# Keys made once a batch for the second cross attention, and weighted sums three chunks behind the scores

## The reference

```
# first (layer 0): 16 heads; the context is layer-normed, heads of 32 features
# second (layer 1):
qh = (q @ Wq + bq).reshape(B, LQ, 16, 8)      # 8 features a head
kh = (k @ Wk + bk).reshape(B, LKV, 16, 8)
vh = (v @ Wv + bv).reshape(B, LKV, 16, 8)
attn = softmax(qh kh^T / sqrt(8));  out = (attn vh) @ Wo + bo
```

## Time and profile before

| | us |
|---|---|
| median of 3 runs | 667.15 (667.14 to 670.14) |
| profiled execution | 664.66 |
| its span, first to last instruction | 662.9 |
| TensorE busy | 621.5 (94%) |
| VectorE, GpSimd, ScalarE busy | 493.9, 379.3, 353.0 |

### The profile page before, as it was taken

One profiled execution on the slowest core, in us unless ns is written; L12 is line 12 of the kernel. 1 busy time (PEld: TensorE's weight loads), 2 busy tenths in 40 slices (PEclk: granted clock), 3 DMA queues, 4 the chain that ended last, 5 costly groups with the idle time before them and its releaser, 6 DMA issues.

```text
span 662.9 us, 19804 instructions
## 1 busy us (share of the span) xinstructions
PE 621.5 (94%) x8743; PEld 464.5 (70%) x8743; DVE 493.9 (75%) x796; ACT 353.0 (53%) x550; POOL 379.3 (57%) x272
## 2 busy tenths in 40 slices
PE   8889898899999999999898979999999999999997
PEld 4566785677777777777776556677777777777774
DVE  3666738799989889896665764877888988977543
ACT  2065663655646646647354316286586586664443
POOL 1362453388888888574220326078988988955400
PEclk9999999999999999999999999999999999999999
DMA  9600003000000002000032000001101100000000
GB/s 267 244 1 3 3 2 134 2 2 3 2 2 2 2 2 95 4 2 2 1 132 120 1 0 1 1 2 48 48 2 49 48 2 2 2 2 2 2 1 15
DMA packets 4657, 20.87 MB, mean 31 GB/s; under 512 B 500, under 2 KB 756, under 8 KB 4572
## 3 DMA queue, kind: packets, MB, share of 16 engines
q1 hardware_dynamic: 4572, 19.60, 8.8%
HBM read 19.37 MB, written 0.23 MB: 30 GB/s over the span
## 4 chain that ended last, share of the span: by engine, by line
PE 72%; DVE 12%; ACT 8%; issue 5%; POOL 2%; DMA 1%; POOLq 0%; DVEq 0%
PE psum L1125 18%; PE psum L1024 10%; PE psum L1066 5%; PE psum L1073 5%; PE psum L212 5%; PE psum L1068 5%; DVE scratch L1241 3%; PE psum L1003 3%; PE psum L1030 1%; PE psum L241 1%; PE psum L1042 1%; POOL scratch L626 1%; ACT scratch L1159 1%; ACT lv L286 1%; PE psum L1036 1%
## 5 line engine op out<-in xcount | busy, mean ns | idle before, releaser
L1226 POOL TENSOR_TENSOR scratch<-scratch 125x896 bf16<-125x896 f32 x136 | 238.5, 1765 | 117.7 <-ACT scratch L1206 117.5
L1206 ACT ACTIVATE scratch<-psum 125x896 f32<-125x896 f32 x192 | 173.1, 915 | 147.0 <-PE psum L1125 145.8
L1241 DVE TENSOR_REDUCE scratch<-psum 128x1 f32<-128x500 f32 x336 | 209.8, 671 | 14.1 <-PE psum L1024 6.4
L1125 PE MATMUL psum<-scratch 128*125 128x448 bf16 (+2 forms) x624 | 143.6, 355 | 0.5 <-ACT scratch L1206 0.2
L1066 PE MATMUL psum<-tok,scratch 125*128 125x65 bf16 x1344 | 108.9, 195 | 1.8 <-DVE kT L1286 1.8
L1068 PE MATMUL psum<-tok,scratch 125*128 125x64 bf16 x1344 | 108.3, 192 | 0.0
L1066 PEld LDWEIGHTS psum<-tok,scratch 125*128 125x128 bf16 x1344 | 95.3, 97 | 15.6 <-issue 2.6
L1024 PE MATMUL psum<-scratch 128*128 128x500 bf16 x273 | 102.3, 375 | 3.3 <-DVE scratch L1241 2.0
L1068 PEld LDWEIGHTS psum<-tok,scratch 125*128 125x128 bf16 x1344 | 90.2, 99 | 16.1
L1125 PEld LDWEIGHTS psum<-scratch 128*125 128x125 bf16 (+2 forms) x624 | 80.0, 136 | 26.1 <-ACT scratch L1206 0.8
L1226 DVE TENSOR_TENSOR scratch<-scratch 125x896 bf16<-125x896 f32 x56 | 68.6, 1227 | 18.1 <-ACT scratch L1206 17.0
(11 more groups left out here) (337 smaller groups left out, 896.7 us busy)
## 6 DMA issues: line engine op xcount, KB each, us to landing
nrm<-turned_dram SPq DMA_DIRECT2D x8, 750.0 KB, 4.6
raw<-ctx_dram SPq DMA_DIRECT2D x4, 672.0 KB
w_third<-fifth_dram SPq DMA_DIRECT2D x3, 636.0 KB, 5.4
w_third<-third_dram SPq DMA_DIRECT2D x2, 844.0 KB, 21.1
w_third<-third_dram SPq DMA_DIRECT2D x2, 843.5 KB, 19.2
w_fourth<-fourth_dram SPq DMA_DIRECT2D x3, 542.5 KB, 5.7
w_first<-first_dram SPq DMA_DIRECT2D x1, 996.0 KB, 4.8
w_second<-second_dram SPq DMA_DIRECT2D x1, 834.0 KB, 6.7
```

The costliest lines, as they stand in the source:

```text
L1125: mm = nc.tensor.matmul(bank(S + f, HALF, CP), lhs[0:rows, CP * c:CP * c + CP], rhs[0:rows, HALF * f:HALF * f + HALF], start=(rows == 128) ...
L1206: nc.scalar.activation(CR["p"][0:CP, n % RING, :].rearrange("p (f n) -> p f n", f=2), psum[0:CP, S:S + 2, 0:HALF], ACT.Exp).then_inc(self. ...
L1226: ops.tensor_tensor(CR["pl"][0:CP, n % RING, :], CR["p"][0:CP, n % RING, :], p_high(n % RING), ALU.subtract).then_inc(done, 1)
L1241: nc.vector.tensor_reduce(mxp[:, r, t:t + 1], bank(B, TB), X_AXIS, ALU.max).then_inc(self.aux_freed, 1)
```

## The change

`LAG` is 3 in place of 2, for both attentions: the sums of chunk n - 3 follow the scores of chunk n. The mean of the batch before moves with it from step 1 to step 2 on VectorE, and N from step 3 to step 4, ahead of the step's M.

`cross2` (`keyed`) now forms keys, once a batch: K, three fp32 products of the 128 key features with 500 context rows. ScalarE adds the bias and makes the high part, VectorE the low part, and DMAs started by SP copy them within the core's memory: for each of four groups of four heads the 32 key rows are stacked as high, low, high, and a row of ones below (97 rows). The queries are put beside them (high, high, low, shift) by 4 fp32 matmuls with a constant (`spread`). Scores are then one matmul of 224 columns for each group, 4 a chunk. M is 24 products a batch, of 112 queries with 500 rows. K for batch b + 2 stands at steps 7 to 9 of batch b; those of the first two batches in the last batch of `cross1`, three at its steps 0 to 2 and three at 8 to 10. Q moves from step 2 to step 1, M from steps 4 to 10 to steps 2 to 10 (three a step, two at 7 to 9), N is copied by ScalarE and not by VectorE, and chunk 1's low part goes to GpSimd. The bf16 conversion of the context for `cross2` goes away. The query projection for `cross2` has 128 columns instead of 512.

```diff
-        LAG = 2
+        KEYED = [("Q", 0), ("Q", 1)] + [("M", u) for u in range(MAXIMA * TBLK)] + [("A", 0), ("A", 1)]
+        EARLY_KEYS = {CHUNKS * (BATCH - 1) + (0, 8)[kb] + t: (kb, t) for kb in range(2) for t in range(TBLK)}
+        LAG = 3
         SIDE = (0, 1, 7)
-        def low_on_pool(n):
+        def low_on_pool(n, keyed):
+            if keyed:
+                return n % 2 == 0 if n >= CHUNKS * (BATCH - 1) + 3 else n % CHUNKS not in (0, 11)
...
+        def keyed_placement(front, outputs, keys):
+            at = [[] for _ in range(CHUNKS)]
+            maxima = iter(KEYED[2:2 + MAXIMA * TBLK])
+            def some(c, n):
+                at[c] += [[u] for u in itertools.islice(maxima, n)]
+            if front:
+                at[1] += [KEYED[0:2]]
+                some(2, 3)
+                some(3, 1)
+            if front:
+                some(3, 2)
+            if outputs:
+                at[4] += [[("N", 0)], [("N", 1)]]
+            if front:
+                for c in range(4, 11):
+                    some(c, 2 if c in (7, 8, 9) else 3)
+                at[11] += [[], [KEYED[-2]], [KEYED[-1]]]
+            if outputs:
+                at[5] += [[("O", 0)]]
+            if keys:
+                for t in range(TBLK):
+                    at[7 + t] += [[("K", t)]]
+            return at
+        def placement(front, outputs):
             at = [[] for _ in range(CHUNKS)]
             if front:
-                if turns:
-                    at[0] += [[FRONT[0]]]
-                    at[1] += [[FRONT[1]]]
+                at[0] += [[FRONT[0]]]
+                at[1] += [[FRONT[1]]]
                 at[2] += [FRONT[2:4]]
                 for c in range(4, 11):
                     at[c] += [[u] for u in FRONT[3 * c - 8:3 * c - 5]]
                 at[11] += [[], [FRONT[25]], [FRONT[26]]]
             if outputs:
-                at[3] += [[], [("N", 0)], [("N", 1)]]
+                at[4] = [[("N", 0)], [("N", 1)]] + at[4]
...
+                    if self.keyed:
+                        for g in range(GROUPS):
+                            mm = nc.tensor.matmul(psum[0:96, self.home(idx + g // 2), 224 * (g % 2):224 * (g % 2) + 224],
+                                                  par("spread", 96 * g, 96 * g + 96), qT[:, :, 56 * b:56 * b + 56],
+                                                  start=True, stop=True)
+                            if g % 2:
+                                mm.then_inc(self.aux_ready, 1)
+                        return
                     for n in range(8):
...
+                elif kind == "K":
+                    mm = self.keys_pe(pe, b, k, B)
+                elif kind == "M" and self.keyed:
+                    t, r = k // MAXIMA, k % MAXIMA
+                    if k == 0 and b:
+                        self.wait_freed(pe, self.index("Q", 1, b))
+                    elif k == 0:
+                        pe.wait_ge(self.front_low, 2)
+                    if r == 0 and t != 1:
+                        pe.wait_ge(keys_loaded[i][t // 2], 192 * (b // 2 + 1))
+                    mm = nc.tensor.matmul(bank(B, TB, QROWS), CR["qa", i][0:96, QROWS * r:QROWS * r + QROWS],
+                                          key_group(i, r // 2)[0:96, TB * t:TB * t + TB], start=True, stop=True)
...
+            def keys_pe(self, pe, b, t, B):
+                if b == 0:
+                    pe.wait_ge(loaded["keys"], 16)
+                pe.wait_ge(turned_loaded[t], 16 * (b + 1))
+                return nc.tensor.matmul(bank(B, TB), par("x_wk"), turned[:, TB * t:TB * t + TB],
+                                        start=True, stop=True)
+            def keys_act(self, act, b, t, B):
+                cols = slice(TB * t, TB * t + TB)
+                if b:
+                    act.wait_ge(keys_loaded[(b - 1) % 2][t // 2], 192 * ((b - 1) // 2 + 1))
+                nc.scalar.activation(key_high[:, cols], bank(B, TB), ACT.Identity, bias=col("x_bk")
+                                     ).then_inc(keys_high, 1)
+            def keys_dve(self, dve, b, t, B):
+                cols = slice(TB * t, TB * t + TB)
+                dve.wait_ge(keys_high, TBLK * b + t + 1)
+                nc.vector.scalar_tensor_tensor(key_low[:, cols], bank(B, TB), col("x_bk"), key_high[:, cols], ALU.add,
+                                               ALU.subtract).then_inc(keys_low, 1)
             def wait_low(self, pe, n):
-                on_pool = low_on_pool(n)
...
+                    if self is cross1 and n == CHUNKS * (BATCH - 1) + 3:
+                        pe.wait_ge(keys_low, TBLK)
...
-                    y = self.context_of(b)
-                    for lhs, rhs, rows in ((CR["ya", y], CR["qa", i], 128), (CR["yb", y], CR["qb", i], below)):
+                    if self.keyed:
+                        if c == 0:
+                            self.wait_freed(pe, self.index("A", 1, b))
+                            pe.wait_ge(self.front_low, 2)
+                            pe.wait_ge(ones_loaded, 32)
+                        for g in range(GROUPS):
+                            mm = nc.tensor.matmul(psum[0:CP, S + g // 2, 224 * (g % 2):224 * (g % 2) + 224],
+                                                  key_group(i, g)[0:97, CP * c:CP * c + CP],
+                                                  CR["qa", i][0:97, 224 * g:224 * g + 224], start=True, stop=True)
+                    for lhs, rhs, rows in () if self.keyed else ((CR["ya", i], CR["qa", i], 128), (CR["yb", i], CR["qb", i], 65)):
...
+                    if self is cross1 and n in EARLY_KEYS:
+                        kb, t = EARLY_KEYS[n]
+                        if kb:
+                            self.wait_freed(pe, self.index("O", 0, BATCH - 2))
+                        cross2.keys_pe(pe, kb, t, SIDE[t]).then_inc(keys_made, 1)
+                if self is cross1:
+                    pe.wait_ge(keys_low, 2 * TBLK)
...
+                elif kind == "K":
+                    act.wait_ge(self.aux_ready, idx + 1)
+                    self.keys_act(act, b, k, B)
+                elif kind == "N" and self.keyed:
+                    act.wait_ge(self.aux_ready, idx + 1)
+                    if k == 0 and b:
+                        act.wait_ge(self.aux_ready, self.index("O", 0, b - 1) + 1)
+                    lo, hi = (0, 512) if k == 0 else (512, 896)
+                    nc.scalar.activation(usb[0:64, lo:hi], bank(B, hi - lo, 64), ACT.Copy).then_inc(self.mean_turned, 1)
...
+                    if self is cross1 and n in EARLY_KEYS:
+                        kb, t = EARLY_KEYS[n]
+                        cross2.keys_dve(dve, kb, t, SIDE[t])
...
+            def keys_in(b, part):
+                cols = slice(2 * TB, CTX) if part else slice(0, 2 * TB)
+                for g in range(GROUPS):
+                    rows = slice(32 * g, 32 * g + 32)
+                    for k, keys in enumerate((key_high, key_low, key_high)):
+                        sp.dma_start(key_group(b % 2, g)[32 * k:32 * k + 32, cols], keys[rows, cols]
+                                     ).then_inc(keys_loaded[b % 2][part], 16)
...
+            for b in range(2, BATCH):
+                for t in range(TBLK):
+                    sp.wait_ge(keys_low, TBLK * b + t + 1)
+                    if b < BATCH - 1:
+                        turned_in(b + 1, t)
+                    if t:
+                        sp.wait_ge(cross2.scores, CHUNKS * (b - 2) + 4 * t + 4)
+                        keys_in(b, t - 1)
```

349 lines of the change are left out of this document (182 added, 167 removed).

## The result

The changed kernel takes 690.84 us (690.76 to 691.54, four runs) against 667.33 (667.14 to 670.14): a ratio of 1.034, 95% interval 1.032 to 1.037. I had forecast 680, in a range of 664 to 689. The sign was right; the size was not. The profiled execution of it has a span of 689.1 us against 662.9, so the two traces are 26.2 apart where I had summed 12.75.

A forecast was written before the change was run, and what follows sets the result against it. TensorE bounds the kernel before; after the change VectorE's chain leads the second attention's middle batches. Terms 10.5 - 0.3 - 1.1 - 4.9 + 1.75 - 0.7 + 4.2 + 3.3 = +12.75, added to the 667.15 median: 680 us, range 664 to 689.

The forecast's parts named there:

- the price of the key steps: Second attention's middle batches: VectorE waits 0.8, 0.55 and 0.55 us at the keys for product, arrival and ScalarE's copy.
- the moved chunk: First attention: one chunk's sums leave batch 0 for a tail that waits for the last exp anyway, -0.7 us.
- (A): TensorE stays the bound and side steps are hidden: 24.7 us for second-attention batches 1 to 5, 656.5 total; chance 0.18.
- (C): Keys come late in the second attention: maxima wait for DMAs paced by SP's starts, 695 us; chance 0.08.
- The slack of zero: Second attention: key DMAs land 10.2 us (5.6 starts, 4.6 landing) after step 8's keys, when maxima read them; cost 0.
- (B): Distance of three is free in the first attention, the mean hidden: +0.7 a batch becomes 0, 675.8 us; chance 0.13.
- Middle batches, +2.1 forecast: Second attention, batches 1 to 5: next scores start at 27.55 us instead of 25.45, five times +2.1, +10.5.
- The timetable: Second attention's middle batch from its first scores: last sums end at 5.3, first reduction at 6.95, fourth maximum waits until 7.0.
- TensorE busy near 23.5: Named check: the second attention's middle batches would be 27.5 us long with TensorE busy near 23.5.
- First attention, +6.8 forecast: First attention: +4.2 us for batches 1 to 6, -0.7 for batch 0's moved sums, +3.3 for batch 7.
- Batch 7, -4.9 forecast: Second attention's last batch, without maxima: 16.1 us where it took 21.0 before, -4.9.
- Front, +1.75 forecast: Second attention's front: three more reductions 1.8, query subtraction 0.6 instead of a 0.5 copy, fewer projections 0.3 back; +1.75.

The follow-up runs named there:

- experiment 5: Changed kernel with key products made from the upper halves of the fp32 words read as bf16 (less exact keys): 688.3 us, ratio 1.031.
- experiment 9: Changed kernel with short key products and no key DMAs, 679.3 us; fp32 products with keys through DRAM, 689.8; short products through DRAM, 678.0.
- experiment 2: Kernel before with only the distance of three (LAG = 3, transposes of the mean in step 4), without keys: 672.30 us, ratio 1.006.
- experiment 6: Changed kernel with each fp32 key product of batches 2 to 7 issued twice into the same bank: 706.1 us, ratio 1.057.

## Why the prediction was right in sign and short in size

The step that failed is the price of the key steps in a middle batch of the second attention. I had VectorE starved for 0.80, 0.55 and 0.55 at the three keys; it is starved for 1.12, 0.74 and 0.74. With the other small errors of a middle batch that makes +1.0 a batch, 5.0 of the 13.4 that lie between the two traces beyond my sum, and the largest part of them. Two steps failed in kind: the keys' high part waits for the DMAs that read it (first attention), and the moved chunk, which I took as a credit there, is a cost. The rest follows part by part.

- **Which rival won: none.** (A) is out: TensorE's busy time in a batch of 28.5 is 25.9, and 28.55 is no sum of its work. (C) I gave 0.08 and 695. In the changed kernel the DMAs cost 1.4 us in batches 1 to 5 and about 1 in the first attention's last, so as a price it is wrong. The slack of zero that I had worked out was right (experiments 5 and 9), but by luck of two errors that cancel: 7.6 + 3.3 and not 5.6 + 4.6. (B) is out (experiment 2).
- **Middle batches, +2.1 forecast, +3.1 without DMA waits: the mis-sized term.** The timetable held to 0.1 up to the fourth maximum: reciprocal at 5.4 after the first scores, first reduction over at 6.9. Then starvation was 0.84 more, the 23 reductions 0.25 more (0.61 each). Of the 0.84, 0.70 is in the key steps: arrival and ScalarE's copy with its bias (0.72 from start to start) were taken from the bf16 query copies of 448 columns. The key steps' price was the steep one, since nearly all of it counts: +0.82 for a longer product and -0.71 for a shorter one (experiments 5, 6 and 9). For five batches that is 5.0; batches 0 and 6 another 0.4, DMA waits 1.4, the dip of the clock 1.1: within 0.2 the 8.1 of the table. The check that I had named, TensorE busy near 23.5, was ill chosen: busy time counts each record 0.16 past its issue, and reads 25.9.
- **First attention, +6.8 forecast, +9.7.** A middle batch takes +0.75 (26.38 against 25.63), where I had +0.7. The distance of three alone makes the whole attention 5.3 longer (experiment 2) where my terms gave 4.2 - 0.7 = 3.5: less six times 0.75 that leaves +0.8 for batch 0 and the tail, where I had a credit of 0.7. The remaining 1.1 is ScalarE's wait to overwrite the keys' high part until the DMAs that read it have landed; I had costed the wait of the scores for the keys, not that of the keys for the DMAs. Starts of both sets fill SP's queue from 311 to 329 us:

```profile
322.93 1.42 SPq L2101
...
328.18 1.89 DMA nrm<-scratch
...
330.15 0.69 ACT scratch L1123
330.87 0.75 DVE scratch L1129
```

- **Batch 7, -4.9 forecast, -3.1.** TensorE does a chunk in 1.06, as summed (646.80 to 647.85, 647.85 to 648.91). Waits for the mean and the output product were 1.1 longer, and the tail is 3.3, not 2.6, since the last low parts run on VectorE and GpSimd at once (below).
- **Front, +1.75 forecast, +1.4**: right, though its own terms (1.8 + 0.6 - 0.5 - 0.3) add to 1.6 and not 1.75. **Clock**: 2.05 that I had at nothing; the rows of before have no dip, and I priced idle time of TensorE as if it were only idle. Since the forecast was added to a median whose executions have dips too, this part belongs to the 26.2 between the traces and not to the 23.5.
- The distance of three itself: I charged the second attention for a mean ahead of its reductions. It is there (idle 1.42 ahead of it) and worth 0.3 to 0.5 a batch. I did not see that the same distance splits TensorE's idle time: its middle batches have no dip, and with distance two every other one has.

## What to carry to other kernels

Where two engines take turns, a product that a third engine has to copy before the second may use it costs its whole length, however idle every engine looks: price it as a chain, start to start, and not by shares. Count the DMA starts on one queue as work of that queue. When one bound is removed and nothing moves, look for a second close to it before giving up the first: here only the run without both told. And look at the granted clock of a batch before explaining why it is longer than its neighbour, and at the clock of the other executions before calling a dip an effect of the change.
